# Flamingo block with gated cross-attention and experts: the bf16 splits of the attention operands move from DVE to ACT and Pool

## What is computed

```
h  = layernorm(x)
y  = causal_attention(h Wq + bq, h Wk + bk, h Wv + bv)            # 16 heads of 16, 512 keys
y += attention(h Wcq + bcq, ctx Wck + bck, ctx Wcv + bcv)         # 1601 keys
x1 = x + tanh(g_xattn) * (y Wp + bp)
n  = layernorm(x1)
out = x1 + tanh(g_ffn) * (shared_swiglu(n) + top-4-of-32 experts(n), capacity 4096)
```

## Time and profile before

| | |
|---|---|
| median of 3 runs | 4883.7 us (4883.43 to 4888.83) |
| the profiled execution | 4891.12 us |
| its span in the profile | 4888.3 us |
| granted TensorE clock over the span | 0.961 of full speed |
| PE, DVE, ACT, POOL busy over the span | 4346.4, 3532.4, 2694.8, 1646.7 us |

### The profile page before, as it was taken

How to read it: one execution, slowest core, us unless ns; L and a number is a source line. 1 busy time by engine, 2 the same in 40 slices (tenths; PEclk the granted TensorE clock), 3 DMA queues, 4 the chain that set the end, 5 groups by cost and what they waited for, 6 DMA issues and landing times. The chain is left out here.

```text
span 4888.3 us, 75159 instructions
## 1 busy us (share of the span) xinstructions
PE 4346.4 (89%) x25317; PEld 1904.0 (39%) x25317; DVE 3532.4 (72%) x7733; ACT 2694.8 (55%) x5523; POOL 1646.7 (34%) x2163
## 2 busy tenths in 40 slices
PE   5999999999999999999999999999999995588882
PEld 2333333333343434333333333333333332477771
DVE  5788788787878787878787877887877783244443
ACT  1665656565655556565656565656565653344441
POOL 1122323232323232323232222323232314388883
PEclk7999999999999999999999999999999997799996
DMA  5453545444444444544444444444444443888888
GB/s 115 71 91 73 111 79 104 81 109 78 106 79 100 79 102 77 109 82 109 82 105 85 98 87 97 83 98 90 97 94 97 93 96 118 178 151 150 149 150 244
DMA packets 363500, 513.22 MB, mean 105 GB/s; under 512 B 64124, under 2 KB 227820, under 8 KB 363176
## 3 DMA queue, kind: packets, MB, share of 16 engines
q1 hardware_dynamic: 272592, 385.16, 37.8%
q0 software_dynamic: 87728, 115.39, 13.3%
q10 hardware_dynamic: 2856, 8.52, 0.5%
HBM read 288.49 MB, written 201.27 MB: 100 GB/s over the span
## 5 line engine op out<-in xcount | busy, mean ns | idle before, releaser
L662 ACT ACTIVATE prob<-scores 128x512 f32<-128x512 f32 (+3 forms) x4352 | 2150.3, 561 | 1331.3 <-PE scores L467 1297.4
L849 DVE TENSOR_REDUCE pmx<-ring 128x1 f32<-128x512 f32 (+1 forms) x3328 | 1998.5, 661 | 188.9 <-PE ring L545 175.6
L467 PE MATMUL scores<-stacks 98*128 98x512 bf16 (+3 forms) x4352 | 1272.3, 369 | 70.5 <-ACT prob L662 41.1
L489 PE MATMUL outs<-prob,vt 128*32 128x512 f32 x8704 | 1096.7, 576 | 12.7 <-POOL prob L1051 11.7
L545 PE MATMUL ring<-stacks 96*128 96x512 bf16 x3072 | 984.4, 389 | 90.1 <-DVE pmx L849 80.7
L467 PEld LDWEIGHTS scores<-stacks 98*128 98x128 bf16 (+1 forms) x4352 | 338.5, 99 | 1244.3 <-ACT prob L662 718.7
L849 DVE TENSOR_REDUCE mc<-ring 128x1 f32<-128x128 f32 (+3 forms) x1024 | 437.1, 480 | 147.1 <-PE ring L562 112.1
L1573 POOL DMA_INDIRECT scratch_sums<-e_yo,e_tok x320 | 495.9, 1550 | 118.8 <-issue 86.2
L1051 POOL TENSOR_SCALAR_AFFINE_SELECT prob<-prob 128x512 f32<-128x512 f32 x256 | 167.9, 656 | 1077.0 <-ACT prob L662 1075.2
L545 PEld LDWEIGHTS ring<-stacks 96*128 96x128 bf16 x3072 | 303.2, 99 | 511.4 <-DVE pmx L849 243.8
L1121 POOL TENSOR_TENSOR split<-rest,split 128x512 bf16<-128x512 f32 (+1 forms) x224 | 218.5, 975 | 824.4 <-DVE split L943 823.9
(11 more groups left out here) (165 smaller groups left out, 3752.7 us busy)
## 6 DMA issues: line engine op xcount, KB each, us to landing
stacks<-scratch_parts SPq DMA_DIRECT2D x768, 128.0 KB, 7.1
stacks<-scratch_parts SPq DMA_DIRECT2D x384, 136.1 KB, 10.1
scratch_parts<-split SPq DMA_DIRECT2D x64, 768.0 KB, 4.5
e_xin<-scratch_slots SPq DMA_DIRECT2D x160, 289.0 KB
scratch_parts<-split SPq DMA_DIRECT2D x32, 816.8 KB, 4.4
num<-oc POOLq DMA_DIRECT2D x256, 64.0 KB
den<-scratch_inverses POOLq DMA_DIRECT2D x63, 256.0 KB, 8.9
ct<-in_ctx_t_dram SPq DMA_DIRECT2D x16, 800.5 KB, 8.2
```

Of the source, the lines that this page charges most:

```text
L467: eng.matmul(ps[0:m, k, q0:T], kst[g][0:KR + 2, j, k0:k0 + m], qst[g][0:KR + 2, j, qc + q0:qc + T], start=True, stop=True).then_inc(scored ...
L489: mm = eng.matmul(po[32 * j:32 * j + 32, q0:T], vt[ch][0:m, VW * vi + VE * hl:VW * vi + VE * hl + 32], prob[0:m, n % 2, j, q0:T], start=kt ...
L662: eng.activation(prob[0:m, n % 2, j, q0:T], ps[0:m, i % SB, q0:T], ACT.Exp, scale=SCALE).then_inc(exped.sem, 1)
L849: eng.tensor_reduce(dst, src, AX.X, ALU.max).then_inc(free_of(part, it), 1)
```

## The change

In the passes F and M, ACT writes the fp32 sum of a split into `rest` and then the first bf16 part, both from PSUM, and the second of these frees the ring bank; before it, it waits on `low` for the split two earlier. DVE does nothing for a split. POOL subtracts the first part from `rest` in place, casts the result to the second part, and forms the third. P keeps the old way. The counts of the events `top` and `middle` follow. In the plan a split's cost is 1.0, not 1.8, so the maxima are dealt otherwise between the places.

```diff
--- before.py
+++ after.py
@@ -187,9 +187,9 @@
     if more:
         deal(0, (42, 54, 47, 53, 55, 56), [("load_x",), ("load_ctx",), ("stats1",), ("norm1",)]
              + [("trans", "ln1", kc) for kc in range(KC)], 0.5)
-        deal(0, (57, 60, 63, 66, 69, 72, 75), split_items(0), 1.8)
+        deal(0, (57, 60, 63, 66, 69, 72, 75), split_items(0), 1.0)
         deal(HALF, range(24, 41, 4), value_items(0), 1.35)
-        deal(HALF, range(47, 66, 3), split_items(1), 1.8)
+        deal(HALF, range(47, 66, 3), split_items(1), 1.0)
     if fin:
         deal(HALF, (9, 10, 11, 12, 13, 14, 15, 16, 17, 18, 19, 22, 23, 24, 25), ROUTE, 1.0)
         deal(HALF, range(28, 28 + len(SCATTER)), SCATTER, 0.0)
@@ -350,13 +350,13 @@
 
         exped = event("exped", **each(4 * SLOTS))
         copied = event("copied", **each(8))
-        top = event("top", P=14, F=14, M=14)
+        top = event("top", P=14)
         row0 = event("row0", P=1, F=4, M=4, L=3)
         tanhed = event("tanhed", M=2, L=2, X=2)
         soft = event("soft", M=1, L=1, X=1)
         gated = event("gated", P=1)
 
-        middle = event("middle", P=14, F=14, M=14)
+        middle = event("middle", P=14, F=28, M=28)
         whole = event("whole", P=1, F=4, M=4, L=3)
         ln = event("ln", by=1, P=9, F=9, M=18, L=9, X=9)
         guess = event("guess", P=1, F=1, M=2, L=1, X=1)
@@ -693,8 +693,13 @@
                         if ch == 1:
                             act.wait_ge(scattered, part, 16)
                         act.wait_ge(routed, part, 40 * ch)
+                    done = top
+                    if part.kind != "P":
+                        done = freed[bank_of(part, it)]
+                        act.wait_ge(low, part, no - 1)
+                        eng.activation(rest[:, no % 2, 0:n], pm[:, bank_of(part, it), 0:n], ACT.Identity, bias=bcol[:, i, ch:ch + 1])
                     eng.activation(split[piece % 2][:, at:at + n], pm[:, bank_of(part, it), 0:n], ACT.Identity,
-                                     bias=bcol[:, i, ch:ch + 1]).then_inc(top.sem, 1)
+                                     bias=bcol[:, i, ch:ch + 1]).then_inc(done.sem, 1)
                 elif what == "shift":
                     g = it[1]
                     full(act, part, it)
@@ -931,7 +936,7 @@
             def second(part, it):
 
                 what = it[0]
-                if what == "split":
+                if what == "split" and part.kind == "P":
                     ch, kind = it[1], it[2]
                     i, wt_, n0, n, at, piece, no = split_of(ch, kind)
                     dve.wait_ge(top, part, no + 1)
@@ -1116,9 +1121,17 @@
                 if what == "split":
                     ch, kind = it[1], it[2]
                     i, wt_, n0, n, at, piece, no = split_of(ch, kind)
-                    mid, last = (split[piece % 2][:, r * SW + at:r * SW + at + n] for r in (1, 2))
-                    pool.wait_ge(middle, part, no + 1)
-                    eng.tensor_tensor(last, rest[:, no % 2, 0:n], mid, ALU.subtract).then_inc(low.sem, 1)
+                    high, mid, last = (split[piece % 2][:, r * SW + at:r * SW + at + n] for r in range(3))
+                    left = rest[:, no % 2, 0:n]
+                    if part.kind == "P":
+                        pool.wait_ge(middle, part, no + 1)
+                    else:
+                        read(pool, part, it)
+                        eng.tensor_tensor(left, left, high, ALU.subtract).then_inc(middle.sem, 1)
+                        pool.wait_ge(middle, part, 2 * no + 1)
+                        eng.tensor_copy(mid, left).then_inc(middle.sem, 1)
+                        pool.wait_ge(middle, part, 2 * no + 2)
+                    eng.tensor_tensor(last, left, mid, ALU.subtract).then_inc(low.sem, 1)
                 elif what == "outproj" and it[1] == NQ - 1:
                     inverse_root(part, "x1")
```

## The result

The change took 4904.5 us (median of 8 runs, 4898.4 to 4909.6) against 4886.3 us for the kernel before beside it (8 runs, 4877.7 to 4891.0): a ratio of 1.0039, 95% interval 1.003 to 1.0048. It is 18 us slower, more than the 0.2% that can be told from no change, where the forecast was 21 us faster. The time lies inside the range. The profiled execution took 4904.7 us, 13.5 more than that of before, and its span is 4902.7.

A forecast was written before the change was run, and what follows sets the result against it. TensorE was taken as the bound, busy 235.8 of 251.4 us a pass. Per pass -4.7 gains + 0.8 ACT + 2.1 POOL + 0.4 store = -1.4 us, -21 us over 15 passes: 4863 us, range 4826 to 4908.

The forecast's parts named there:

- the end of the pass: Last slots: POOL's longer chain delays the mask, weighted sums 2.6 us late; cost 2.1 us a pass, bounds 1.5 to 3.0.
- some 0.5 us of waits that follow: Existing PE waits after the late weighted sums at the pass's end, expected to be swallowed by the delay.
- the deal: Cost 1.0 moves maxima towards the splits; gains 0.8 at routing, 1.1 after it, 0.4 us in places 31 to 56.
- I take 2.4: First split stretch, places 57 to 75: PE gains 2.4 us a pass from DVE's relief, bounds 0.3 to 2.7.
- ACT's second activation: An extra 0.687 us per large split delays exponentials; cost 0.8 us a pass, bounds 0 to 8.9.
- PE's idle time: Claimed ceiling: all another engine can give back is what PE waits, 15.6 us of a pass.
- The chain's three durations: POOL's three instructions per large split: 1.2, 0.7 and 1.089 us, 3.2 us with hand-overs.
- the maxima waits: Sign named in advance: PE's waits for the maxima go down by a third.
- 0.4 us later ... on the path: First half's last piece: its store, waiting for POOL's small chain, comes 0.4 us later, bounds 0 to 1.0.
- Rival 1: Slower, chance 0.27: POOL's chain of 3.9 us ahead of the masks decides; +2.1 us a pass, 4915 us.
- Rival 3: Much faster, chance 0.12: weight-load waits are real stalls, 8 of 17.8 us come back; -4.7 us a pass, 4813 us.
- The page: Skill's advice: keep elementwise work on VectorE, GpSimd about twice as slow for two inputs; by it the change would lose.

The follow-up runs named there:

- pool_late_end: Kernel before, with POOL's one subtraction for the split of place 130 made three times in a chain: 4950.91 us, ratio 1.0108.
- change_again: The change unaltered, run again on another chip: 4920.14 us, ratio 1.0045 to the kernel before.
- engines_only: The change with the plan's cost of a split put back to 1.8: 4931.78 us, ratio 1.0066 to the kernel before.
- half: Kernel before with routing steps two places later, first half's splits the new way, second half's the old, cost 1.8: 4815.47 us, ratio 0.9834 to the kernel before.
- pool_late_else: Kernel before, with POOL's subtraction tripled in the 11 large splits other than that of place 130: 4897.23 us against 4833.44, ratio 1.0134.

## Why the prediction was wrong

**Two terms of the sum failed, and either alone takes the forecast gain to nothing.** The first is the end of the pass. "Cost 2.1 us a pass, bounds 1.5 and 3.0" stood for the masks behind POOL's chain. The place was right, the chain took 3.0 us (3.2 forecast), and the weighted sums came 2.2 us late (2.6 forecast). Even "some 0.5 us of waits that follow" were swallowed: 0.7 us of them are gone, and PE's idle time rose by 1.35 us only. What the sum had no term for is the clock behind the stand. PE is busy 2.2 us longer a pass for the same work, with 78.5 us at half the clock where there were 6.8. The end cost 3.5 us, outside its bounds. pool_late_end shows the whole of it with nothing else changed, and the two ends of the kernel before show what the clock does alone: 1.6 us in one end. By the table's spread between executions the 3.5 may be 3.2.

**The second is the deal, which was priced on one side.** The prediction took 0.8, 1.1 and 0.4 from the stretches that lose maxima and nothing for those that get them. By change_again less engines_only the losing stretches (28 to 57, 77 to 96, 96 to 115) gave 0.55, 1.35 and 0.59 us, together 2.5 where 2.3 were taken. Places 57 to 77 lost 1.15 of it and places 115 to 130 another 0.70. Net it gave 0.65, about 10 us in 15 passes, as the ratios have it. The two kernels ran on different chips, so only the losses in the split stretches are firm.

**What held.** "I take 2.4" for the first split stretch and 0.8 for ACT's second activation make -1.6 us a pass together. Measured together in the two split stretches it is -1.7 (engines_only and half), all in the first. No run parts the two. PE's idle time was no ceiling for the gain, as the prediction had it: 1.4 of the 1.7 us came off its busy time. The chain's three durations are right within 0.1 us. By the signs named in advance: DVE's wait for ACT is gone and the mask waits rose by 1.8 us a pass at the last slots, both as said; the maxima waits fell by 18% and not by a third.

**What stays open.** "0.4 us later ... on the path" stood for the last piece's store. DVE's wait for it (L871) is 36.1 us in engines_only against 27.3 in pool_late_end, 0.6 a pass, within the bounds of 0 and 1.0, and places 77 to 115 are 0.7 us longer. But moving the routing steps away from that wait gained no more in the changed kernels (40 and 35 us) than without the change (48), and the two stretches differ by as much between executions.

**The sum.** Taken: -1.6 for the split stretches with ACT, +0.4 store, +2.1 end, -2.3 deal, together -1.4. Measured: -1.7, +0.7, +3.5, -0.7, together +1.8, where the two ratios of the change (19 and 22 us) say 1.3 to 1.5; the rest is the spread between executions. Of the 3.2 us between forecast and outcome the deal is 1.6, the end 1.4, the store 0.3, and the split stretches give 0.1 back. Put into the forecast by itself, the measured end makes it 0 and the measured deal +0.2.

**The rivals.** Rival 1 had the side and nearly the time (4915), but not its condition: it needed a chain of 3.5 us or more, and took 2.1 us at the masks of the first split stretch. The chain was 3.0 us and PE waited for no mask there. That this rival had the side is luck: more than half of the end's cost came by the clock, which it didn't name. Rival 3 took the weight loads' waits for real stalls of 8 us. Stalls outside PE's idle time there were, but the whole gain of the split stretches was 1.7.

**The page.** POOL's two-input subtraction takes 1.16 us, DVE's took 0.75, a factor of 1.5, though DVE's instruction was another: it also added the bias and read PSUM. The Trainium skill, "GPSIMD Engine Reference", section Engine selection, keeps such work on VectorE for a factor of about 2; this case doesn't reach that factor. By the runs the place decides, not the factor: one such chain ahead of a mask costs 3.5 us a pass, and the seven splits of the first half, moved alone, gain 2.6 us a pass (39 / 15, from half).

## What to carry to other kernels

Before work is moved to an idle engine, list what stands behind it in that engine's queue and in the DMA queues that it releases, place by place; here the last large split of a pass cost more than the others gave, and moving only the first seven won 39 us. Price a new stand of TensorE above its length: here the clock fell behind it in every pass, and that cost more than the stand. When maxima or other filler are dealt anew, price the stretch that gets them as well as the one that loses them.

## What the runs showed of the hardware

- **Chips differ by more than the change.** The kernel before takes 4833 us on one chip and 4886 to 4900 on the others. Places 96 to 115 of one pass by windows, of the kernel before and then of pool_late_else on the fast chip, whose code is the same there:

```profile
1276.71:1309.29 32.58, 29.95 (x215) 12.99 (x211) 25.63 (x59) 18.36 (x41) 21.24 (x26) 1.00 0.44 112
```

```profile
1291.24:1320.21 28.97, 28.90 (x214) 13.26 (x211) 25.46 (x59) 18.25 (x41) 21.23 (x26) 1.00 0.48 121
```

DVE does the same work in both, and PE lacks 2.6 us in one and 0.1 in the other. All four kernels on that chip take 29.0 to 30.0 us for these places, the other thirteen traces 31.4 to 34.3. So these gaps, which the prediction had put down to DVE's lateness, were not DVE's alone, and the verdicts above rest on ratios within one chip.
